# Keys and queries of a two-layer attention block go from SBUF to SBUF into their stacks, with no copy in the device's memory

## The reference, cut to what matters

```python
x = x + tanh(g_xattn[0]) * xattn0(layernorm(x), ctx, ctx, mask, W_q, W_k, W_v, W_proj, b_proj)
x = x + tanh(g_ffn[0])   * ffn0(layernorm(x), w_gate, w_up, w_down)
x = x + tanh(g_xattn[1]) * xattn1(layernorm(x), ctx, ctx, ..., Wq, Wk, Wv, Wo, bo)
x = x + tanh(g_ffn[1])   * moe1(layernorm(x), w_router, w_gate, w_up, w_down)
# xattn: q, k, v = projections, 16 heads of 16
#   softmax(q k^T / 4 [masked in layer 0]) v, then the output projection
```

## Time and profile before

| | us |
|---|---|
| median of three runs | 1337.96 (1337.96 to 1345.0) |
| the profiled execution, its own time | 1334.98 |
| its span, first to last instruction | 1333.7 |
| PE busy in it | 1193.3 (89%), granted clock 0.956 |
| DVE, ACT, POOL busy | 896.2, 711.2, 479.3 |
| queue q1 (what SP issues) | 91,696 packets, 151.40 MB |

### The profile page before, as it was taken

How to read it: one execution, slowest core, us unless ns; L and a number is a source line. 1 busy time by engine, 2 the same in 40 slices (tenths; PEclk the granted TensorE clock), 3 DMA queues, 4 the chain that set the end, 5 groups by cost and what they waited for, 6 DMA issues and landing times.

```text
span 1333.7 us, 24380 instructions
## 1 busy us (share of the span) xinstructions
PE 1193.3 (89%) x8913; PEld 825.2 (62%) x8913; DVE 896.2 (67%) x2671; ACT 711.2 (53%) x1192; POOL 479.3 (36%) x675
## 2 busy tenths in 40 slices
PE   4789999999999959998978988999899899857998
PEld 3467776767667634443437865666666676536997
DVE  2668777777777646599897946767867868642333
ACT  1255565555555539888763416566566565522221
POOL 5344443344432100166000333343633643322555
PEclk8799999999999979999988988999999999977999
DMA  5655455544563050000004664766666655136983
GB/s 153 149 126 132 120 128 144 132 120 117 132 149 87 18 167 0 1 1 1 0 1 142 186 150 119 172 170 169 169 185 159 156 133 131 50 133 197 313 214 39
DMA packets 101457, 162.33 MB, mean 122 GB/s; under 512 B 10833, under 2 KB 89803, under 8 KB 95173
## 3 DMA queue, kind: packets, MB, share of 16 engines
q1 hardware_dynamic: 91696, 151.40, 43.3%
q0 software_dynamic: 7296, 8.15, 3.3%
q10 hardware_dynamic: 2346, 1.22, 0.4%
HBM read 108.75 MB, written 52.53 MB: 121 GB/s over the span
## 4 chain that ended last, share of the span: by engine, by line
PE 42%; DVE 9%; DMA 7%; issue 6%; POOL 3%; ACT 3%; SPq 1%; ACTq 0%; POOLq 0%; DVEq 0%
PE PS L569 10%; PE PS L609 5%; PE PS L582 4%; PE PS L323 4%; PE PS L383 4%; DMA QS<-qd 3%; DMA qd<-PP 3%; PE PS L342 3%; PE PS L366 3%; PE PS L618 2%; PE PS L415 2%; DVE AM L1241 2%; PE PS L441 1%; DVE NM L969 1%; PE PS L330 1%
## 5 line engine op out<-in xcount | busy, mean ns | idle before, releaser
L714 ACT ACTIVATE P<-PS 128x512 f32<-128x512 f32 x512 | 302.4, 601 | 168.1 <-PE PS L369 99.0
L966 DVE CUSTOM_DVE_ANT_0 MX<-PS,NQ 128x256 bf16<-128x256 f32 x512 | 192.7, 418 | 70.5 <-PE PS L342 70.2
L366 PE MATMUL PS<-QS,KS 99*128 99x256 bf16 x1024 | 228.2, 276 | 9.2 <-ACT P L714 7.7
L342 PE MATMUL PS<-KS,QS 96*128 96x256 bf16 x1024 | 201.1, 279 | 34.0 <-DVE NM L966 13.9
L969 DVE TENSOR_REDUCE NM<-PS 128x2 f32<-128x512 f32 x256 | 173.9, 686 | 79.4 <-PE PS L342 76.4
L342 PEld LDWEIGHTS PS<-KS,QS 96*128 96x128 bf16 x1024 | 86.6, 98 | 105.5 <-DVE NM L969 29.1
L383 PE MATMUL PS<-P,V 128*32 128x256 f32 x2048 | 138.2, 388 | 1.7 <-ACT P L714 1.7
L366 PEld LDWEIGHTS PS<-QS,KS 99*128 99x128 bf16 x1024 | 95.7, 100 | 55.5 <-ACT P L714 22.6
L369 PE MATMUL PS<-NK,identb 128*128 128x256 bf16 x512 | 129.2, 277 | 0.0
L569 PE MATMUL PS<-XNT,wup 128*128 128x512 f16 x576 | 126.2, 382 | 0.0
L569 PEld LDWEIGHTS PS<-XNT,wup 128*128 128x128 f16 x576 | 56.5, 98 | 68.5 <-issue 1.9
(11 more groups left out here) (230 smaller groups left out, 2414.3 us busy)
## 6 DMA issues: line engine op xcount, KB each, us to landing
kd<-PP SPq DMA_DIRECT2D x32, 384.0 KB
KS<-kd SPq DMA_DIRECT2D x32, 384.0 KB, 4.7
qd<-PP SPq DMA_DIRECT2D x32, 384.0 KB, 4.9
QS<-qd SPq DMA_DIRECT2D x32, 384.0 KB, 4.6
WH<-in_wex SPq DMA_DIRECT2D x16, 768.0 KB
KS<-kd SPq DMA_DIRECT2D x32, 256.0 KB, 5.3
QS<-qd SPq DMA_DIRECT2D x32, 256.0 KB, 5.3
WG<-in_wex SPq DMA_DIRECT2D x10, 768.0 KB
```

The source lines that it names most:

```text
L342: ins = tensor.matmul(PS[:, bk, 256 * qt:256 * qt + 256], t.QS[b % 3][0:96, h, 128 * qt:128 * qt + 128], t.KS[b % 3][0:96, h, :], start=Tr ...
L366: ins = tensor.matmul(o, t.KS[b % 3][0:99, h, 128 * kt:128 * kt + 128], t.QS[b % 3][0:99, h, :], start=True, stop=(L == 1))
L714: scalar.activation(t.P[h % 8][:, :, :], PS[:, h % 2, :].rearrange("p (k n) -> p k n", k=2), ACT.Exp).then_inc(s_ex, 1)
L966: ins = vector.tensor_tensor_reduce(t.MX[:, 2 * (h % 2) + qt, :], PS[:, bk, 256 * qt:256 * qt + 256], t.NQ[b % 4][:, qt, :], -1.0, 1.0e30, ...
```

## The change

`sp_parts` and the two tensors in the device's memory are gone, and so are their semaphores. `sp_stack` now takes one part of one sequence: it waits for that part (`s_hi`, `s_mid` or `s_lo`) and sends it from `PP` straight into the stack, once for every group of rows that holds it, six transfers of 128 KB a stack (the high part three times, the middle part twice, the low part once). The groups are no longer blocks of 16 rows: group j is rows j, j + 6, j + 12 and so on to j + 90, and `MIX` says which part is in which group, for keys and for queries, so that the same six products are added. Each transfer has 16 destination rows of eight pieces of 1 KB; the source is the 128 partitions of one part. Keys are sent at kk = 2 (high) and 3, queries at kk = 4 (high) and 6. ACT, before it overwrites the high part, waits for all six transfers of the previous sequence's stack; PE waits for six transfers a stack (96). In `PP` the parts stand in one order for both.

```diff
+MIX = ((0, 1, 2, 0, 1, 0), (2, 1, 0, 1, 0, 0))
...
-            pe.wait_ge(d_qs[b % 3], 48 * uses(L, b, 3))
-            pe.wait_ge(d_ks[b % 3], 48 * uses(L, b, 3))
+            pe.wait_ge(d_qs[b % 3], 96 * uses(L, b, 3))
+            pe.wait_ge(d_ks[b % 3], 96 * uses(L, b, 3))
...
             scalar.activation(t.QF, v, ACT.Copy, scale=scale)
-            act.wait_ge((d_kw, d_qw)[which], 16 * n)
-            scalar.activation(PP[1 - which][:, place(which, 0), :, :], v, ACT.Copy, scale=scale).then_inc(s_hi, 1)
+            if n:
+                act.wait_ge((d_ks, d_qs)[which][(b - 1) % NB % 3], 96 * uses((n - 1) // NB, (b - 1) % NB, 3))
+            scalar.activation(PP[1 - which][:, 0, :, :], v, ACT.Copy, scale=scale).then_inc(s_hi, 1)
...
-            for row, k in ((0, 3), (48, 2), (80, 1)):
-                first = 3 - k if which else 0
-                sync.dma_start(dst(row, k), src[first:first + k].rearrange("s r n -> (s r) n")).then_inc(stacked[b % 3], 16)
+        def sp_stack(L, b, which, part):
+
+
+            i = 2 * (L * NB + b) + which
+            st, stacked = ((TL[L].KS, d_ks), (TL[L].QS, d_qs))[which]
+            sp.wait_ge((s_hi, s_mid, s_lo)[part], i + 1)
+            sp.wait_ge(s_s, 16 * (L * NB + b - 2))
+            sp.wait_ge(s_st, 16 * (L * NB + b - 2))
+            for j in range(6):
+                if MIX[which][j] == part:
+                    sync.dma_start(st[b % 3][j:96:6, :, :].rearrange("r (q m) n -> r q (m n)", m=2),
+                                   PP[1 - which][:, part, :, :].rearrange("p m n -> p (m n)")).then_inc(stacked[b % 3], 16)
...
-                if kk == 3:
-                    sp_parts(L, b, 0)
-                if kk == 5:
-                    sp_stack(L, b, 0)
-                if kk == 6:
-                    sp_parts(L, b, 1)
-                if kk == 8:
-                    sp_stack(L, b, 1)
+                for part in range(3):
+                    if kk == (2, 3, 3)[part]:
+                        sp_stack(L, b, 0, part)
+                    if kk == (4, 6, 6)[part]:
+                        sp_stack(L, b, 1, part)
```

More of the change, by code:

```diff
@@ L60, in rows @@
     return d[b * S:(b + 1) * S, :].rearrange("(t p) d -> p t d", p=128)
-def place(which, part):
-    return 2 - part if which else part
+MIX = ((0, 1, 2, 0, 1, 0), (2, 1, 0, 1, 0, 0))
 def uses(L, b, k):
@@ L102, in build @@
         x1d, x2d = dram("x1d", (T, D), F32), dram("x2d", (T, D), F32)
-        qd, kd = dram("qd", (3, 3, 256, 256), BF16), dram("kd", (3, 3, 256, 256), BF16)
         bufd = dram("bufd", (EC, D + 2), F32)
@@ L262, in build @@
         d_w = {n: sem("d_w" + n) for n in "qkvo"}
-        d_qw, d_kw = sem("d_qw"), sem("d_kw")
         d_qs, d_ks = ([sem(f"d_{w}s{i}") for i in range(3)] for w in "qk")
@@ L974, in dve_mid @@
             dve.wait_ge(s_r1, i + 1)
-            vector.tensor_copy(PP[1 - which][:, place(which, 1), :, :], TL[L].R1).then_inc(s_mid, 1)
+            vector.tensor_copy(PP[1 - which][:, 1, :, :], TL[L].R1).then_inc(s_mid, 1)
         def dve_any(b):
@@ L1434, in pool_rest @@
             pool.wait_ge(s_lo, i)
-            gpsimd.tensor_tensor(t.R1, t.QF, PP[1 - which][:, place(which, 0), :, :], ALU.subtract).then_inc(s_r1, 1)
+            gpsimd.tensor_tensor(t.R1, t.QF, PP[1 - which][:, 0, :, :], ALU.subtract).then_inc(s_r1, 1)
         def pool_low(L, b, which):
@@ L1439, in pool_low @@
             pool.wait_ge(s_mid, i + 1)
-            gpsimd.tensor_tensor(PP[1 - which][:, place(which, 2), :, :], t.R1, PP[1 - which][:, place(which, 1), :, :], ALU.subtract).then_inc(s_lo, 1)
+            gpsimd.tensor_tensor(PP[1 - which][:, 2, :, :], t.R1, PP[1 - which][:, 1, :, :], ALU.subtract).then_inc(s_lo, 1)
         def pool_masks(b):
```

## The result

The changed kernel takes 1320.61 us, the median of four runs (1319.07 to 1322.39). Beside it the kernel before took 1340.32 us (1337.96 to 1345.0). The ratio is 0.9858, with a 95% interval of 0.9833 to 0.9883: it is faster by 19.7 us. Forecast were 1329.0 us and 1322 to 1338. One execution of the kernel before, which took 1760.8 us at a granted clock of 0.65, is left out of all that follows.

A forecast was written before the change was run, and what follows sets the result against it. PE was taken to bound the kernel (busy 1193.3 of 1333.7 us), so only its idle time for the replaced transfers could be won: -5.5 - 2.0 - 1.5 = -9.0 us, from 1337.96 to 1329.0 us, range 1322 to 1338.

The forecast's parts named there:

- term 3: Start of layer 0: sequence 3's mask lands sooner behind lighter queues, sparing PE's wait near 73 us; -1.5 us (0 to -1.9).
- term 1: Layer 1, sequences' first scores: PE's seven waits for the queries' stack, 5.9 us, vanish; -5.5 us (-2.5 to -6.7 with weight loads).
- the distance of 2.98 us between profile and median: Whole kernel: runs' median stands 2.98 us above the profiled 1334.98, so the forecast starts from 1337.96.
- term 2: Layer 0's first scores: stack some 8 us earlier removes PE's 2.06 us idle, mask also sooner; -2.0 us (0 to -2.1).
- rival B: Gain taken back as waits for maxima and exponentials; 2 to 6 us remain, 1334 us; chance 0.22.
- A: All sequences: small transfers fill the queues, 2.2 us more in some 14 sequences of layer 1; 1367 us; chance 0.10.
- about 2 in two of them: Layer 1: the queries-to-scores loop outlasts PE's own work by 0.4 us in most sequences, about 2 in two.
- Terms 4 and 5: SP's twelve issues per sequence for eight, and ACT's new wait before overwriting the high part: 0 each (term 4 up to +0.5).
- the room of 8 us: Layer 1: the queries' stack is there at 884.8, PE asks at 892.9; cover 8 us, 5 at the upper bound.
- Rival C: Lighter queues also speed later masks and rows and the start of layer 1; -13 us, 1325 us; chance 0.13.

The follow-up runs named there:

- first pair: The kernel before and the changed kernel as first measured and profiled: medians 1340.32 and 1320.61 us, profiled executions 1334.98 and 1322.39 us.
- the repetition: Both kernels run and profiled once more with no edit: the kernel before 1341.15 us, the changed kernel 1321.23 us.
- second pair: Traces of the kernel before and the changed kernel, each run again with no edit: 1341.15 and 1321.23 us.
- late with new transfers (105.4): Changed kernel with all six transfers of a stack waiting for the low part: 1331.59 us; 4th projection of values starts at 105.4 us.
- early with old ones (96.2): Kernel before with rows, context and masks of layer 0's sequences 2 and 3 issued four slots earlier: 1331.57 us; 4th values' projection at 96.2.

## Why the prediction was right and wrong

**What failed.** The sum of 9.0 us was too small in term 3 (1.5 us for some 7), in term 1 (5.5 for 7.5 and 11.2), and in the distance of 2.98 us between profile and median, which was added as a constant; term 2 was wrong in its mechanism.

**The mechanism of term 1 held, its size did not.** All waits for `QS` in layer 1 went, and nothing took their place, as forecast; rival B is refuted (waits for maxima stayed at 8.5 and 8.4 us from the 17th to the 32nd landmark), and A (twelve transfers fill the queues) too: the DMA share of a sequence fell from 0.66 to 0.47. Forecast 5.5 us, measured 7.5 in the first pair and 11.2 in the second. Two errors lie in it. The 5.9 us were read from PE's own list; PE's weight loads waited 8.6 us in layer 1 for the same transfers, in ten places and not seven, and the loads are what the next matmul needs: that list, which I gave the upper end of the term only, is near the 7.5. Sequence by sequence the loss against after is the wait of the load less about 0.1 us (2.4 for 2.55, 2.0 for 2.10). And the 5.9 are one execution's draw from landings that vary; the repetition had 10.5 by the loads and gained 11.2, since one sequence lost 4.6 us for a wait of 3.03, at the lower clock behind it. The "about 2 in two of them" is a property of the loop by its place, but not by its size.

**Term 2 failed in its mechanism.** The first scores indeed started without a wait, at 33.93, but PE then stood 3.11 us until 37.64. DVE's cast of the middle part of the next queries, done at 36.91, stands in program order ahead of the first row maxima, and PE's fifth group of scores waits for a maximum (before, the cast was done at 35.99, under PE's wait for the stack). The repetition agrees: in all four traces the fifth group starts 1.1 to 1.2 us after the cast does (36.73, 37.64, 36.39, 35.88), whether PE waited for the stack before it or not. The 2nd landmark moved by 0.9 us later in the first pair and 0.5 earlier in the second. The mask did land sooner, DVE had it at 43.39 for 44.90 (forecast 42.9), and that was worth something later on: it belongs to the next term.

**Term 3 was mis-sized, 1.5 us for 7.0.** The mask of sequence 3, issued at 60.62, was taken up at 65.77, after 5.2 us (forecast 6 between bounds that it calls fastest and median; 4.1 is the median of the earlier trace rows, 8.2 this very mask), and PE's 1.87 us at 73.04 went. But the term counted one wait of PE. PE's waits for maxima between the 2nd and the 4th landmark fell by 4.9 us, and the clock was not in the sum at all: 3.0 us of the 7.0 in the first pair, 5.3 of the 8.0 in the second, by PE's busy time. The row was there: the earlier trace rows had the first 100 us at a clock of 0.86.

**Terms 4 and 5 held.** An issue takes 0.64 to 0.74 us (3.85 and 4.45 us for six), not the 0.41 of the earlier trace rows, so SP pays 8 us a sequence and not 4.9; it stays hidden. No wait of ACT for the stacks appears on the chain. The landing was taken as 3 us and is 2.4; the room of 8 us was real (7.9): 4.7 us of delay cost nothing, 9.0 cost 1.1 a sequence.

**The sum.** It gave 9.0 for the 12.6 us between the two profiled executions: 7.0 between the 2nd and 4th landmark, less 0.9 ahead of it, 7.5 in layer 1, less 1.0 elsewhere. The other 7.1 us of the 19.7 lie between those executions and the medians: the one of before was 5.3 us quicker than its median beside the changed kernel, the one of after 1.8 slower. I put the median's distance on top as if it were a constant, and as 2.98 us, where the later runs have 5.3. A good part of it is what the removed waits and the clock behind them vary by: layer 1 takes 352.2 to 356.2 us in the four traces with the old way there, and 344.0 to 345.1 in the six with the direct transfers and no wait for them. The rest of the distance was not traced. Rival C ("more than PE's waits", -13) was the nearest, with masks and start in it, but named the start of layer 1, which gained nothing (33.6 us before and after), and had 0.13.

**The queues and the place of the masks.** For the first mask the traces settle what the start gained by: it was issued at 38.80 us before and 40.31 after (38.59 and 38.54 in the second pair), no earlier, and DVE took it up 6.1 and 3.1 us later (5.6 and 3.0). That is the lighter queue ahead of it, as terms 2 and 3 had it. The second mask was issued 2.8 us sooner (3.5) and taken up 3.0 us sooner after its issue (4.5). Its issue in the kernel after, beside 63.41 in the earlier trace rows:

```profile
60.62 0.41 SPq L1583 DMA_DIRECT2D MM<-in_mm  x1
```

**Left open.** Why the second mask is issued sooner was not taken apart: it can be the place in SP's order or only the start running ahead. That the place alone can decide is shown by two kernels: late with new transfers (105.4) and early with old ones (96.2).

## What to carry to other kernels

Size the gain of a removed wait by the weight loads' list as well as the matmuls', and by more than one execution: if the removed transfer varies, a part of the spread of the runs belongs to the gain. Look at the granted clock behind a wait of PE, and compare PE's busy time for the same matmuls. Compare waits between landmarks of the work and not between fixed times, or an event that moved out of the window reads as a gain. And where a store becomes several issues, ask first what stands behind them in the queue; in a steady loop only the moment of landing counts, and holding one transfer back step by step measures its room.

## What the runs showed of the hardware

- A transfer of 128 KB from SBUF to SBUF in pieces of 1 KB lands in 2.4 us into 16 rows six apart, and in 6.0 us into 16 neighbouring rows (medians of the queries' stack from issue to landing, sent up to six behind one another; for keys 2.8 and 4.9). The DMA engines are busy for 0.44 and 0.70 of the time with it, at 121 and 124 GB/s.
- After a wait of 1.87 us the matmuls of the kernel before ran from 75.1 to about 79 us at 0.21 us a piece in place of 0.11. A wait of 2.75 us in its repetition was followed by a granted clock of 0.69 for 4 us, one of 2.72 in the same execution by none below 1.00.
- Steady sequences of layer 1 bore 222 GB/s (787 to 1130 us, with the old traffic added) where the kernel before moved 157 and the changed one 121, and lost 1.7 us in 13 of them.
- An issue whose destination is a pattern of 16 x 8 pieces takes SP 0.64 us and more; one of 128 plain rows 0.41 to 0.63.
